# Gates of x from TensorE for half of the rows, and x loaded later

## The reference, cut to what matters

```python
x = x + gnn0(layernorm(x))     # A @ (ln @ W0 + b0) / deg, A is 4096 x 4096 of 0 and 1, x is 4096 x 256
x = x + ffn(layernorm(x))      # logits = ln(x) @ Wg + bg; top 2 of 8 experts per row; gelu MLPs
x = x + gnn1(layernorm(x))     # normalised adjacency, then relu(... @ WL + bL)
x = x + lookup(layernorm(x))
```

## Time and profile before

| | |
|---|---|
| median of three runs | 1023.33 us |
| the profiled execution: its time, its span | 1023.41 us, 1021.6 us |
| mean granted clock of PE | 0.957 |
| busy: PE, DVE, ACT, POOL | 925.5, 628.3, 401.2, 429.5 us |
| matmuls of the four sweeps (L1006) | 1024, 237.1 us busy |
| DVE's products for the gates of x (L628) | 256, 125.6 us busy |
| chain that ended last | PE 23%, DVE 2%, issue 1% of the span |

### The profile page before, as it was taken

How to read it: one execution, slowest core, us unless ns; L and a number is a source line. 1 busy time by engine, 2 the same in 40 slices (tenths; PEclk the granted TensorE clock), 3 DMA queues, 4 the chain that set the end, 5 groups by cost and what they waited for, 6 DMA issues and landing times. The chain is left out here.

```text
span 1021.6 us, 21589 instructions
## 1 busy us (share of the span) xinstructions
PE 925.5 (91%) x6509; PEld 605.7 (59%) x6510; DVE 628.3 (62%) x2051; ACT 401.2 (39%) x837; POOL 429.5 (42%) x435
## 2 busy tenths in 40 slices
PE   7999899999913899999999999999379999999994
PEld 4344344544502899989899889889234454444442
DVE  7617999998698655655655656656256141241644
ACT  5868829575896443233233232233013101010111
POOL 4446707704676245545545545545444400210110
PEclk9999999999955999999999999999789999999997
DMA  9999959889786423323322332323299979875770
GB/s 332 404 319 358 365 187 358 323 307 374 263 289 180 162 44 48 53 46 47 53 46 46 54 47 44 56 47 47 44 329 402 371 233 324 272 258 171 241 257 29
DMA packets 91434, 199.92 MB, mean 196 GB/s; under 512 B 14097, under 2 KB 47122, under 8 KB 91250
## 3 DMA queue, kind: packets, MB, share of 16 engines
q1 hardware_dynamic: 74626, 169.41, 47.1%
q0 software_dynamic: 16752, 29.82, 14.5%
HBM read 177.04 MB, written 22.16 MB: 195 GB/s over the span
## 5 line engine op out<-in xcount | busy, mean ns | idle before, releaser
L1006 PE MATMUL bank<-adj_f,feat 128*128 128x512 f16 x1024 | 237.1, 388 | 7.3 <-DMA adj_f<-in_adjT 5.3
L1259 ACT ACTIVATE act_f<-bank,b_sb 128x256 f32<-128x256 f32 (+1 forms) x312 | 122.2, 449 | 255.4 <-PE bank L1190 255.4
L1190 PE MATMUL bank<-rT,experts 128*128 128x256 f16 (+1 forms) x1872 | 191.2, 263 | 2.4 <-DVE rT L1298 2.4
L1202 PE MATMUL bank<-experts,act_h 128*128 (+1 forms) x1680 | 189.1, 273 | 0.0
L1660 PE MATMUL bank<-adj_g,feat 128*128 128x512 f16 x768 | 179.7, 388 | 1.5 <-POOL feat L1486 1.5
L1190 PEld LDWEIGHTS bank<-rT,experts 128*128 (+1 forms) x1872 | 168.8, 99 | 19.8 <-DVE rT L1298 2.9
L1006 PEld LDWEIGHTS bank<-adj_f,feat 128*128 128x128 f16 x1024 | 97.8, 96 | 136.0 <-DMA adj_f<-in_adjT 7.4
L1202 PEld LDWEIGHTS bank<-experts,act_h 128*128 128x128 f16 x1680 | 163.0, 98 | 18.2
L1117 POOL DMA_INDIRECT x_rows<-y,token x70 | 116.0, 1657 | 66.1 <-issue 57.9
L891 ACT ACTIVATE spent<-adj_f 128x1024 f16<-128x1024 f32 x128 | 135.1, 1055 | 13.6 <-DMA adj_f<-in_adjT 6.7
L1660 PEld LDWEIGHTS bank<-adj_g,feat 128*128 128x128 f16 x768 | 74.4, 97 | 94.8 <-issue 2.4
(11 more groups left out here) (261 smaller groups left out, 977.6 us busy)
## 6 DMA issues: line engine op xcount, KB each, us to landing
adj_f<-in_adjT SPq DMA_DIRECT2D x128, 512.0 KB, 7.0
adj_g<-in_adjT SPq DMA_DIRECT2D x72, 512.0 KB, 6.1
adj_early<-in_adjT SPq DMA_DIRECT2D x24, 512.0 KB, 7.0
adj_g<-in_adjT SPq DMA_DIRECT2D x48, 256.0 KB, 3.1
unit_f<-in_W SPq DMA_DIRECT2D x16, 512.0 KB, 6.9
stage<-in_W SPq DMA_DIRECT2D x12, 512.0 KB, 6.2
x_ring<-in_x POOLq DMA_DIRECT2D x16, 256.0 KB, 6.5
x_rows<-agg SPq DMA_DIRECT2D x4, 1024.0 KB, 9.7
```

What stands on the lines that cost most here:

```text
L1006: last = pe.matmul(mine(s)[ib * DC + c][:, :], feat0[:, j, h, c * P:(c + 1) * P], adj_0[j % RING][:, ib * HALF_SWEEP:(ib + 1) * HALF_SWEEP ...
L1190: last = pe.matmul(pb[2 + q][:, k * SLOT + at:k * SLOT + at + width], w1_part(mine_e * DC + (f // FQ * W2_UNIT0 + c), wh)[:, (f % FQ) * P: ...
L1202: last = pe.matmul(pb[6 + r][:, 0:D], act_h[:, ah, f, r * P:(r + 1) * P], experts[:, ds(e[r] * DC + (W2_UNIT0 + f // UH), 1), wh, (f % UH) ...
L1259: last = a.activation(act_f[q][:, k, at:at + width], pb[2 + q][:, k * SLOT + at:k * SLOT + at + width], ACT.Gelu, bias=b1_sb[:, ds(mine_e ...
```

## The change

The 32 tiles are divided. For tiles 16 to 31 DVE makes the products as before (128 instructions). For tiles 0 to 15 PE does: behind the first and second pair of matmuls of the tiles 22 to 29 of sweep 0 it transposes the four feature blocks of one row tile (two rows for each adjacency tile), DVE copies the result to SBUF (`take_transposed`), and one place later PE multiplies it with a centred Wg in float16 halves, `wgx16` (`gate_row`, four matmuls of 16, 8, 16 and 8 columns). DVE reads all of these sums once, ahead of sweep 1, whose banks they share.

With this, five other things move. `load_gate_rows` goes from SP's queue to POOL's, its first half behind unit 1 and the last `gate_row`, its second behind unit 2. On DVE `turn_gate_rows` comes behind `low_sums(0)`, and no products are ahead of `take_rows` in sweep 1, 16 instructions in sweep 2. Rows go out behind tiles 8 to 15 in sweeps 1 and 2, behind 20 to 27 only in sweep 3. x's pieces are loaded behind tiles 0, 3, 7 and 12. PE's opening run of dummy matmuls has 90 in place of 70. An eight-column load (`wg_end`) and three small instructions of DVE make `wgx16`.

```diff
+    xT = [w(f"xT{i}", [P, 2, DC, P], F16) for i in range(2)]
-    ROWS_OUT_AT = 20
+    XT_FROM, XT_EACH, XT_TILES, ROWS_OUT_AT, ROWS_OUT_LAST = 22, 2, NT // 2, 8, 20
-    X_AFTER = {0: 1, 2: 2, 5: 3, 7: 4}
+    X_AFTER = {0: 1, 3: 2, 7: 3, 12: 4}
...
-                    if (s, j) == (1, 4):
-                        sp.wait_ge(sem("w_lo_ready"), 2)
-                        sp.wait_ge(sem("w0g_ready"), 2)
-                        sp.wait_ge(sem("spare_zeroed"), 32)
-                        load_gate_rows(0)
-                    if (s, j) == (1, 6):
-                        sp.wait_ge(sem("wg_half_turned"), 1)
-                        load_gate_rows(1)
...
-            for u in range(W2_UNIT0):
+            for u in range(2):
                 split_unit(u)
             pool.wait_ge(sem("spare_zeroed"), 32)
+            pool.wait_ge(sem("w_lo_ready"), 2)
+            pool.wait_ge(sem("w0g_ready"), 2)
+            pool.wait_ge(sem("xT_used"), XT_TILES)
+            load_gate_rows(0)
+            split_unit(2)
+            pool.wait_ge(sem("wg_half_turned"), 1)
+            load_gate_rows(1)
+            for u in range(3, W2_UNIT0):
+                split_unit(u)
...
+            def take_transposed(n):
+                v.wait_ge(sem("xT_ps_ready"), n + 1)
+                if n >= 2:
+                    v.wait_ge(sem("xT_used"), n - 1)
+                v.tensor_copy(xT[n % 2][:, :, :, :].rearrange("p h c n -> p (h c n)"), pb[4 + n % 2][:, 0:D].bitcast(F16)
+                              ).then_inc(sem("xT_ready"), 1)
...
             take_w0T()
             split_w0()
-            split_w0g()
-            for h in range(2):
-                turn_gate_rows(h)
+            for n in range(XT_TILES):
+                take_transposed(n)
+                if n == 9:
+                    split_w0g()
+            take_x_gates()
+
+            BESIDE, BEHIND = 2, 5 * E
+            low_sums(0)
+            turn_gate_rows(0)
+            take_numbers()
+            turn_gate_rows(1)
             total_gate_rows()
-            BEFORE, BESIDE, BEHIND = 16, OT, 5
             done = 0
             for s in (1, 2):
-                if s == 1:
-                    x_gates(0, 2)
-                    low_sums(0)
-                    take_numbers()
-                    x_gates(2, BEFORE)
-                else:
-                    low_sums(s - 1)
-                    x_gates(done, done + BEFORE)
-                done += BEFORE
+                if s == 2:
+                    low_sums(1)
+                    x_gates(done, done + 2 * E)
+                    done += 2 * E
                 for k in range(OT):
                     take_rows((s - 1) * OT + k)
-                    x_gates(done + k, done + k + 1)
-                x_gates(done + BESIDE, done + BESIDE + BEHIND)
-                done += BESIDE + BEHIND
+                    x_gates(done, done + BESIDE)
+                    done += BESIDE
+                x_gates(done, done + BEHIND)
+                done += BEHIND
...
+            def transpose_row(n):
+                pe.wait_ge(sem("hid_lo_ready"), n + 1 + 2)
+                if n >= 2:
+                    pe.wait_ge(sem("xT_ready"), n - 1)
+                dst = pb[4 + n % 2][:, 0:D].bitcast(F16).rearrange("p (h c n) -> p h c n", h=2, c=DC)
+                for h in range(2):
+                    for c in range(DC):
+                        last = pe.transpose(dst[:, h, c, :], feat0[:, n, h, c * P:(c + 1) * P], ident16[:, :])
+                last.then_inc(sem("xT_ps_ready"), 1)
+
+            def gate_row(n):
+                pe.wait_ge(sem("xT_ready"), n + 1)
+                k = 0
+                for c in range(DC):
+                    for h, width in ((0, 2 * E), (1, E)):
+                        last = pe.matmul(pb[6][:, n * 2 * E:n * 2 * E + width], xT[n % 2][:, h, c, :],
+                                         wgx16[:, c, :, :].rearrange("p h e -> p (h e)")[:, 0:width],
+                                         start=(k == 0), stop=(k == 3))
+                        k += 1
+                last.then_inc(sem("xT_used"), 1)
...
-            for _ in range(70):
+            for _ in range(90):
...
+                def row_gates(k):
+                    n = (j - XT_FROM) * XT_EACH + k
+                    if k < XT_EACH and n < XT_TILES:
+                        transpose_row(n)
+                    if k < XT_EACH and 0 < n <= XT_TILES:
+                        gate_row(n - 1)
+
+                tile_sums(0, j, row_gates if j >= XT_FROM else None)
                 weight_work(j)
...
                 if s == 1:
+                    pe.wait_ge(sem("xg_read"), 1)
                     pe.wait_ge(sem("w0g_ready"), 2)
...
-                at = ROWS_OUT_AT
+                at = ROWS_OUT_LAST if s == NS - 1 else ROWS_OUT_AT
```

More of the change, by code:

```diff
@@ L232, in program @@
     wg_sb = w("wg_sb", [P, DC, E], F32)
+    wg_end = w("wg_end", [P, E], F32)
+    wgx = w("wgx", [P, DC, E], F32)
+    wgx16 = w("wgx16", [P, DC, 2, E], F16)
     wgc = w("wgc", [P, DC, E], F32)
@@ L587, in centre_weights @@
                 v.tensor_copy(ident16[:, :], ident[:, :]).then_inc(sem("ident16_ready"), 1)
+                v.tensor_tensor(wgx[:, :, :], wg_sb[:, :, :], wg_end[:, :].unsqueeze(1).broadcast_to([P, DC, E]), ALU.subtract
+                                ).then_inc(sem("wgx_ready"), 1)
+                v.wait_ge(sem("wgx_ready"), 1)
+                v.tensor_scalar(wgx16[:, :, 0, :], wgx[:, :, :], WS, None, ALU.mult).then_inc(sem("wgx_ready"), 1)
+                v.wait_ge(sem("wgx_ready"), 2)
+                v.scalar_tensor_tensor(out=wgx16[:, :, 1, :], in0=wgx[:, :, :], scalar=WS, in1=wgx16[:, :, 0, :],
+                                       op0=ALU.mult, op1=ALU.subtract).then_inc(sem("wgx_ready"), 1)
                 v.wait_ge(sem("wg_sum_ready"), 1)
@@ L621, in x_gates @@
             def x_gates(first, end):
[L622 to L629, removed]
+                for k in range(first, end):
+                    n, e = XT_TILES + k // E, k % E
+                    if k >= PRODUCTS:
+                        v.wait_ge(sem("v_gates"), k - PRODUCTS + 1)
+                    gate_steps.did(v.tensor_tensor_reduce(out=products[:, k % PRODUCTS, :], in0=agg[:, n, :], in1=wg_turned[:, e, :],
+                                                          scale=1.0, scalar=0.0, op0=ALU.mult, op1=ALU.add, accum_out=xg[:, n, e:e + 1]))
@@ new lines, in take_x_gates @@
+            def take_x_gates():
+                st = Steps(v, sem("v_xg"))
+                tiles = slice(0, XT_TILES)
+                v.wait_ge(sem("xT_used"), XT_TILES)
+                sums = pb[6][:, 0:XT_TILES * 2 * E].rearrange("p (n h e) -> p n h e", n=XT_TILES, h=2)
+                st.link(v.tensor_copy(xg[:, tiles, :], sums[:, :, 0, :]))
+                v.tensor_tensor(xg[:, tiles, :], sums[:, :, 1, :], xg[:, tiles, :], ALU.add).then_inc(sem("xg_read"), 1)
+                st.link(v.scalar_tensor_tensor(out=t1[:, tiles], in0=var[:, tiles], scalar=1.0 / WS, in1=r[:, tiles], op0=ALU.mult, op1=ALU.mult))
+                v.wait_ge(sem("xg_read"), 1)
+                v.tensor_tensor(xg[:, tiles, :], xg[:, tiles, :], t1[:, tiles].unsqueeze(2).broadcast_to([P, XT_TILES, E]), ALU.mult
+                                ).then_inc(sem("xg_taken"), 1)
@@ L631, in centre_x_gates @@
             def centre_x_gates():
+                tiles = slice(XT_TILES, NT)
                 v.wait_ge(sem("wg_totalled"), 1)
-                shift = products[:, 0, :].rearrange("p (n e) -> p n e", e=E)
+                shift = products[:, 0, 0:(NT - XT_TILES) * E].rearrange("p (n e) -> p n e", e=E)
                 gate_steps.wait()
-                gate_steps.link(v.tensor_tensor(shift, over_experts(mv0[:, :, 0]), over_tiles(wg_total[:, :]), ALU.mult))
-                v.tensor_tensor(xg[:, :, :], xg[:, :, :], shift, ALU.subtract).then_inc(sem("xg_taken"), 1)
+                gate_steps.link(v.tensor_tensor(shift, mv0[:, tiles, 0].unsqueeze(2).broadcast_to([P, NT - XT_TILES, E]),
+                                                wg_total[:, :].unsqueeze(1).broadcast_to([P, NT - XT_TILES, E]), ALU.mult))
@@ L638, in take_numbers @@
+                v.tensor_tensor(xg[:, tiles, :], xg[:, tiles, :], shift, ALU.subtract).then_inc(sem("xg_taken"), 1)
             def take_numbers():
@@ L734, in _ @@
             low_sums(2)
-            x_gates(done, 2 * NT)
             centre_x_gates()
@@ L1004, in tile_sums @@
                     for c in range(DC):
+                        if between is not None and h + c:
+                            between(h * DC + c - 1)
                         for ib in range(IB):
@@ L1041, in _ @@
             for j in range(NT):
[L1042 removed]
+                if j == XT_FROM:
+                    pe.wait_ge(sem("ident16_ready"), 1)
+                    pe.wait_ge(sem("wgx_ready"), 3)
+                def row_gates(k):
[5 more added lines that the diff above has]
```

(1 more changed line is left out.)

16 lines of the change are left out of this document (9 added, 7 removed).

## The result

Twelve executions of the changed kernel have a median of 1027.32 us, against 1023.88 us for twelve of the kernel before: a ratio of 1.0029, 95% interval 1.0019 to 1.0039, that is 1.9 to 4.0 us slower. One of the twelve took 2512.88 us, at a granted clock of 1.00; nothing on record explains it, and the ratio leaves it out. The forecast was 1026.4 us, 3.0 us above the kernel before; by the ratio it is 3.0 us too. The profiled execution took 1026.58 us, with a span of 1024.8 us against 1021.6.

A forecast was written before the change was run, and what follows sets the result against it. DMA bounds the first part of sweep 0, then PE. Terms -8.0 + 4.1 + 5.3 + 1.3 + 0.2 give +2.9 or 3.0 with roundings, on 1023.41: 1026.4 us; range 1021.6 to 1031.2.

The forecast's parts named there:

- removed: wait and clock in sweep 1: Sweep 1, sixth block of rows out: PE's 6.53 us wait for DVE's first copy and the lower clock go, -8.0 us.
- the wait at tile 22: Sweep 0, first `gate_row`: PE waits 5.5 us for DVE's copy queued behind the splits of W0 and WL; term +4.1 us.
- clock behind it: PE behind the wait at tile 22: lower clock costs between 0 and 1.4 us, taken as +1.3 us.
- the rest of PE's rows: PE's transposes and short matmuls for 16 rows: 5.8 us, less 0.45 already counted, +5.3 us.
- Wg's rows from POOL: Sweep 1, second half of Wg's rows loaded by POOL: cover of about 0.7 us, term +0.2 us.
- 1.2 us late: Sweep 0: the last piece's statistics on DVE, which ACT waits for, come 1.2 us late, and ACT's later work with them.
- the transition: PE's way back from a row's short matmuls into the 512 column matmuls: 0.025 us a row.
- PE at tile 22: Sweep 0: with x's pieces moved, PE is at tile 22 at 54.1, 1.9 us earlier than before.
- The wait without clock: Rival: wait at tile 22 costs no clock or a little less; +1.0 to +2.0 us, about 1024.9; chance 0.25.
- the late rows of Wg: Rival: sweep 1, second half of Wg's rows lands late; at 12 us of landing +5.1 + 1.3, 1032.8; chance 0.12.
- the dear short matmuls: Rival: PE's short matmuls take 56 to 101 ns each; +1.8 to +4.7 us, 1028.2 to 1031; chance 0.11.
- The 63.4 us: Tile 22: time of DVE's copy if VectorE and GpSimd exclude each other; +6.5 in place of +4.1, 1028.8 us; no chance given.

The follow-up runs named there:

- old x: Changed kernel with x's pieces loaded behind tiles 0, 2, 5 and 7 as before the change; ratio 1.0006 to the kernel before.
- pool late: Changed kernel with POOL's splits of units 0 and 1 held until DVE has done W0 and WL; ratio 0.9997 to the kernel before.
- order twice: The `order` kernel with every transpose and every gate matmul of PE issued twice; 1024.09 us, ratio 0.9998 to the kernel before.
- warm: Changed kernel with 44 dummy matmuls of 256 columns on PE ahead of the first `gate_row`; ratio 1.0009 to the kernel before.
- order: Changed kernel with DVE's copies of transposed rows ahead of the splits of W0 and WL; 1019.02 us, ratio 0.9954 to the kernel before.
- balanced: Kernel before with 12 groups of products, not 16, ahead of the first copied block and 9, not 5, behind the last; ratio 0.9979 to it.
- balanced 2: Kernel before with product groups 12 ahead and 9 behind in sweep 1 only, sweep 2 left at 16 and 5; ratio 0.9997 to it.
- the same with x later: The balanced 2 kernel with x's pieces loaded behind tiles 0, 3, 7 and 12; ratio 0.9991 to the kernel before.

## Why the prediction was right

The median came out 0.9 us above the forecast, of which 0.5 is in the base (1023.88 against 1023.41), and the mechanism was the forecast one. By the ratio the two agree to 0.1 us, and that is closer than the terms deserve: their errors are +1.0, +0.55, -0.5 and -0.2 and partly cancel, the sum at L205 is 0.8 us above the forecast, and 0.55 of that is regained behind it. The terms, read at the same places of the trace:

| Term | predicted | measured |
|---|---|---|
| removed: wait and clock in sweep 1 | -8.0 | -8.0 |
| the wait at tile 22: first `gate_row` against 56.87 | +4.1 | +5.1 (61.95) |
| clock behind it | +1.3 | +1.85 |
| the rest of PE's rows | +5.3 | +4.8 (16 x 0.327 - 0.44) |
| Wg's rows from POOL | +0.2 | 0 |
| sum, against L205's 3.75 | +2.9 | +3.75 |

**The wait at tile 22** was right in its place and its chain, and 1.0 us short. The error is in one step, "1.2 us late" for ACT. The piece of tiles 16 to 23 was taken up at 26.28 instead of 25.9, its rows took 4.14 us (3.79 before), the three small operations on 16 columns took 1.35 us instead of 0.6, and the last piece's statistics began at 38.55, 2.6 us later than before:

```profile
26.28 0.42 DVE L553 BATCH_NORM_STATS2 stats<-agg 128x6 f32<-128x256 f32 x1 [2.18 <-issue]
...
37.10 0.65 DVE L594 TENSOR_TENSOR wgx<-wg_sb,wg_end 128x16 f32<-128x16 f32 x1
37.79 0.17 DVE L597 TENSOR_SCALAR wgx<-wgx 128x16 f16<-128x16 f32 x1
38.00 0.53 DVE L599 SCALAR_TENSOR_TENSOR wgx<-wgx,wgx 128x16 f16<-128x16 f32 x1
38.45 0.16 DVE L602 SCALAR_TENSOR_TENSOR wgc<-bank,wg_sb 128x16 f32<-128x16 f32 x1
38.55 0.41 DVE L553 BATCH_NORM_STATS2 stats<-agg 128x6 f32<-128x256 f32 x1
```

Of the three small operations two read two operands from SBUF, and these were the slow ones (0.65 and 0.53 us), with POOL's subtractions for the features beside them (36.17 to 38.50). In old x POOL was idle at that place (33.64 to 34.31), and the three took 0.16, 0.17 and 0.17 us. ACT's root follows at 42.16 (39.57 before) and W0's high half 2.6 us later than before. Against this the two splits took 3.2 us, not 3.6: the first began 0.02 us ahead of POOL's subtraction and ran undisturbed (0.69, where I had 2.07), while POOL took 2.65 against 2.13, and the second took 2.62 where I had 1.52. That the two together came near is luck in part. The short matmuls and the transposes were sized rightly (25 ns for 28, 55 for 56), the transition was a little less.

**PE at tile 22** was to be there at 54.1 and was at 55.30. Tile 8 started at 27.59 (27.4 predicted), but the 24 matmuls from there took 7.20 us in place of 5.59, and the reason is not DMA but the clock (stretches of the profile after):

```profile
27.50:29.00 1.50, 1.41 (x6) 0.63 (x7) 1.48 (x5) 0.00 (x0) 0.00 (x0) 0.85 1.04 423
29.00:31.00 2.00, 2.00 (x7) 0.59 (x6) 1.60 (x12) 1.10 (x3) 0.52 (x1) 0.50 1.02 407
31.00:33.00 2.00, 2.00 (x8) 0.81 (x7) 1.86 (x6) 2.00 (x6) 1.33 (x3) 0.76 1.07 386
```

I had taken waits of 1.9 us for free. Before, PE stood for 1.46 us, worked 1.98 and stood 1.88, and kept its clock; after, it stood 1.14, worked 1.98 and stood 1.98, and lost it. Of the eight profiles with x later, six show this fall behind tile 7, and the two without it (pool late, order twice) have tile 22 at 54.70 and 54.25, near the prediction. Of the five with x as before one shows it, for one tile. That x later causes it is likely by these counts and not shown. The length of the idle time ahead of tile 7 alone does not decide it: behind 0.56 us the clock fell (warm), behind 0.97 us it did not (pool late). In the changed kernel this 1.2 us cost nothing, since PE waited behind it. In `order` it is part of the time: tile 22 starts at 55.67 there.

**Wg's rows.** The first copy of a block ended at 112.0 and PE needed it at 112.77: a cover of 0.8 us, as forecast. The landing took 7.2 us instead of 6.2.

**The rivals.** The wait without clock (warm shows what it would be worth, 1.8 us), the late rows of Wg and the dear short matmuls did not occur. On the split, the Trainium skill ("SBUF — State Buffer", section "Who interferes with whom") has the two instructions exclude each other. Here it depended on what POOL did. Beside its subtraction WL's split ended 0.6 us behind POOL (2.62 us against 0.68 without), which is the rule; beside its scaling in place the split took 1.52 us and ended first, which is not, as far as POOL's recorded times can be trusted. The 63.4 us that I had for the copy by the rule did not come, since POOL's work lay otherwise; with POOL's end at 61.00 as measured the rule gives 61.00 + 0.68 = 61.68 for the end of WL's split, and it was 61.56. It deserved a chance of its own among the rivals.

## What to carry to other kernels

When work is moved to the engine that is the bound, look first at who brings it its operands, and at what stands ahead of that in the helper's queue: the same instructions cost 3 us or brought 5 us depending on whether DVE's copies stood behind or ahead of two instructions that waited for a third engine. A wait on the bound engine costs its own length, and the waits of 2.8 to 7.5 us seen here cost another 1.3 to 2.2 us of lower clock. Moving work about in a full queue moved the wait here and kept at most 2.1 of the 8.0 us (balanced); with 128 or 160 of the 256 products in the queue PE waited for no copied block.

## What the runs showed of the hardware

- The cost of the lower clock did not follow the length of the wait. Behind waits of 2.8, 4.0, 5.1 us (old x, pool late, the changed kernel) it was 1.5, 1.4, 1.85 us, behind 3.25, 6.0 and 7.5 us (balanced, balanced 2, the same with x later) 1.65, 2.2 and 1.5, behind 0.34 (warm) nothing.
- The clock also falls some time after PE has resumed: in old x PE worked again from 60.54, and the granted clock was 0.97 in 60 to 62 us and 0.50 in 62 to 64.
- Short matmuls with a stationary operand of 128 columns each started every 25 ns, and four float16 transposes of 128 columns, interleaved with 512 column matmuls, every 55 ns; with two such rows for each tile the granted clock stayed at 1.00 (68 to 83 us after the change).
